# Front projections in two rounded passes, key weights turned on TensorE, expert gate and up products in three rounded passes

## The chip, the cores and the metric

The kernel runs on one core of one Trainium2 chip. The metric is device time in microseconds (us). The core has five engines that matter here: PE (TensorE, matrix products), DVE (VectorE), ACT (ScalarE), POOL (GpSimd) and SP (SyncE, which only issues DMAs). Each works through its own list of instructions in order and waits on semaphores that other engines raise.

## The reference, cut to what matters

`x` is 256 tokens of 256 numbers (batch 8, length 32). Six layers add to it, one after the other. The change touches three of them.

```
# layer 1: quantised attention over 8 groups of 2 heads, head size 128
xq   = fp8(bf16(clip(ln_out / in_scale)))          # one xq for each of qx, k, v, q
q    = ln((xq * in_scale) @ wq.T * w_scale)        # 2048 columns; the same for qx, k (1024), v (1024)
kx   = ln(cond @ w_kv_x[:1024].T)                  # keys of the cross attention, 8 x 512 context rows
x    = x + (self attention | cross attention) @ wproj
# layer 2: state space layer
# layer 3: eight experts of 256 x 256, two of them used by each token
g = silu(x @ Wg[e]); u = x @ Wu[e]; out += ((g * u) @ Wd[e]) * w_e
# layer 4: attention over the context with a mask; layer 5: rotary attention
# layer 6: FFN whose weights come from a table of 16 values: w = lut[idx]
```

## The kernel before

All 256 tokens stay on chip. Every engine has its own hand-written list; nothing is planned by a program at run time. Four stretches follow each other.

**Front.** Six chunks of projection weights of 1024 columns each (`wch`, two buffers) are loaded in turn: two for qx, one for k, two for q, one for v. `project(n)` (L1500) multiplies a chunk with the fp8-rounded input `xs`, which DVE makes in `scaled_input` (last line L1735) for one of four input scales. Both operands are fp32, so that each product of 512 columns is two instructions on PE. The results go to PSUM banks 0 to 3. ACT copies them out in `read_chunk` (L1612) to `raw`. DVE takes statistics of 16 heads in `norm_heads` (L1756 to L1770) while ACT gives the reciprocal root (`act_rstd`, L283 and L284) in the middle. Then DVE scales the first eight heads (L1775) and ACT the other eight in `normalise` (L1632). PE turns the result by transposes (`turn`, L1514), ACT reads it back with the norm's weights (`read_turn`, L1639), and `cross_queries` (L1524, L1529; copied out at L1621) folds the key weights `wkc` into the cross queries. The order of `norm_heads` and of `normalise` is fixed as chunk 0, 1, 2, 3, 4. The key weights are held twice: `wkc`, centred by PE, and `wkT`, the same weights loaded transposed by a second DMA and centred by DVE (L1743 to L1745). At the end `wkT` is split: ACT rounds it to fp32r (`wk_hi`, L1659), DVE subtracts (`wk_lo`, L1800). A product is then taken in rounded passes (hi by hi, hi by lo, lo by hi), each one fp32r instruction.

**Loop.** Eight context rows pass through `loop_pe`: keys and scores in three rounded passes (L429 to L431), mixes in fp32 (L456). In the meantime ACT (`leaf`, L653), DVE (`term`, L660) and accumulating DMAs issued by POOL (L666) build the table weights `lutw` in eight steps of three parts.

**Experts.** `gate_up` (L1043) is eight fp32 products of 256 columns for one expert; ACT takes the silu (L1198), DVE clamps and multiplies (L1325, L1329), `down` (L1054) multiplies back and DVE adds to `x` (L1337). `gate_up(e)` runs one expert ahead of `down(e-1)`. The last two steps of the table weights are spread over experts 2 to 7. Where PE would be idle, `keep_clock` (L364) issues products whose results nobody reads.

**Rest.** Layers 4, 5 and 6, each a chain of norm, turn, product, softmax.

## Time and profile before

| what | value |
|---|---|
| median of 3 runs | 479.61 us (478.98 to 480.41) |
| time of the profiled execution | 483.38 us |
| its span, first to last instruction | 481.6 us |
| PE busy | 450.2 us (93%) |
| DVE busy | 352.0 us (73%) |
| ACT busy | 248.7 us (52%) |
| mean granted TensorE clock | 0.982 |

The profile is of one execution, 3.77 us longer than the median of the runs; 1.78 us of its time lie outside the span. Busy shares are means over stretches with different limits, so that each stretch has to be read by itself. A granted clock of 1.0 is 2.4 GHz, 0.5 is 1.2 GHz.

### The profile page before, as it was taken

The numbers are of one execution on the slowest core, as the hardware profiler recorded it, in microseconds if no ns is written. First come the engines' busy times: TensorE is split into PE (matmuls) and PEld (weight loads), VectorE is DVE, ScalarE is ACT, GpSimd is POOL, SyncE is SP. The second block draws the span as 40 slices with busy tenths as digits, with TensorE's granted clock in tenths as the row PEclk, the third lists the DMA queues.
The fourth block names the chain that finished last, engine by engine and source line by source line (L and its number), as shares of the span: only waits on it lengthen the run. The fifth ranks groups of instructions, "written<-read, shape, count | busy, mean of one in ns | idle before, by whom it ended". The sixth has DMA issues, their size and how long they took to land.

```text
span 481.6 us, 6644 instructions
## 1 busy us (share of the span) xinstructions
PE 450.2 (93%) x2336; PEld 304.9 (63%) x2342; DVE 352.0 (73%) x729; ACT 248.7 (52%) x784; POOL 25.5 (5%) x33
## 2 busy tenths in 40 slices
PE   5987999989999999999999999998888999989897
PEld 2442445667887676767576776856655888536566
DVE  5888495849799869698899989766776468644731
ACT  1465688997553677758986676553020205110120
POOL 0000000000110000101001010100000111100000
PEclk9999799999999999999999999999998999989999
DMA  8167020224201114693448464880068579720000
GB/s 314 82 228 297 0 88 0 79 99 160 82 0 45 44 45 109 136 319 70 110 109 172 111 131 110 177 333 0 1 206 329 176 206 222 166 85 1 1 1 22
DMA packets 14046, 58.57 MB, mean 122 GB/s; under 512 B 1792, under 2 KB 2496, under 8 KB 12480
## 3 DMA queue, kind: packets, MB, share of 16 engines
q1 hardware_dynamic: 10992, 41.66, 23.6%
q0 software_dynamic: 3024, 16.52, 17.6%
q8 instruction: 17, 0.28, 0.2%
q14 instruction: 13, 0.11, 0.1%
HBM read 41.40 MB, written 0.26 MB: 87 GB/s over the span
## 4 chain that ended last, share of the span: by engine, by line
PE 74%; DVE 12%; ACT 10%; issue 2%; DMA 1%; SPq 0%; DVEq 0%; ACTq 0%
PE PS L456 11%; PE PS L429 9%; PE PS L431 8%; PE PS L430 8%; PE PS L1043 6%; PE PS L1529 3%; PE PS L1500 3%; PE PS L476 3%; PE PS L1054 3%; ACT raw_dt.float L1632 3%; PE PS L503 2%; PE PS L1154 2%; ACT raw_dt.float L1612 2%; PE PS L465 1%; PE PS L364 1%
## 5 line engine op out<-in xcount | busy, mean ns | idle before, releaser
L576 ACT ACTIVATE sq_dt.float<-PS 128x128 bf16<-128x128 f32 x256 | 67.3, 281 | 28.9 <-PE PS L431 22.2
L456 PE MATMUL PS<-s_dt.float,ctx_ring_dt.float 128*128 128x512 f32 x128 | 57.7, 593 | 1.3 <-DVE px_dt.float L810 1.3
L429 PE MATMUL PS<-wkc_dt.float32r,ctx_hi_dt.float32r 128*128 128x512 f32 x128 | 53.7, 420 | 1.6 <-ACT sq_dt.float L576 1.2
L576 ACT ACTIVATION_READ_ACCUMULATOR sq_dt.float<-PS 128x1 f32 x256 | 53.8, 211 | 0.0
L431 PE MATMUL PS<-wkc_dt.float32r,ctxT_ring_dt.float32r 128*128 128x512 f32 x128 | 50.4, 393 | 0.0
L430 PE MATMUL PS<-wkT_dt.float32r,ctx_hi_dt.float32r 128*128 128x512 f32 x128 | 50.1, 392 | 0.0
L653 ACT ACTIVATE luttmp_dt.float<-low_bit_dt.float,vec_dt.float,small_dt.float 128x1536 f32<-128x1536 uint8 x24 | 38.5, 1656 | 10.5 <-DMA lutw_dt.float<-luttmp_dt.float 10.5
L1500 PE MATMUL PS<-wch_dt.float,xs_dt.float 128*128 128x512 f32 x96 | 42.2, 594 | 0.7 <-DVE xs_dt.float L1735 0.7
L456 PEld LDWEIGHTS PS<-s_dt.float,ctx_ring_dt.float 128*128 128x128 f32 x128 | 23.6, 190 | 25.0 <-issue 23.0
L660 DVE SCALAR_TENSOR_TENSOR luttmp_dt.float<-idx_dt.float,luttmp_dt.float 128x1536 f32<-128x1536 uint8 x21 | 36.5, 1750 | 0.0
L364 PE MATMUL PS<-consts_dt.float 128*128 128x512 bf16 x116 | 28.9, 404 | 6.0 <-DMA consts_dt.float<-in_consts 5.5
L429 PEld LDWEIGHTS PS<-wkc_dt.float32r,ctx_hi_dt.float32r 128*128 128x128 f32 x128 | 24.0, 187 | 14.1 <-ACT sq_dt.float L576 9.3
L1500 PEld LDWEIGHTS PS<-wch_dt.float,xs_dt.float 128*128 128x128 f32 x96 | 17.8, 190 | 22.3 <-issue 20.3
L666 POOL DMA_DIRECT2D lutw_dt.float<-luttmp_dt.float x21 | 18.3, 871 | 188.2 <-DVE luttmp_dt.float L660 188.2
L431 PEld LDWEIGHTS PS<-wkc_dt.float32r,ctxT_ring_dt.float32r 128*128 128x128 f32 x128 | 24.0, 188 | 5.7
L430 PEld LDWEIGHTS PS<-wkT_dt.float32r,ctx_hi_dt.float32r 128*128 128x128 f32 x128 | 24.1, 188 | 3.6
L797 DVE TENSOR_TENSOR s_dt.float<-s_dt.float,PS 128x2048 f32<-128x2048 f32 x8 | 18.3, 2288 | 10.3 <-PE PS L446 10.3
L364 PEld LDWEIGHTS PS<-consts_dt.float 128*128 128x128 bf16 x122 | 12.1, 103 | 21.0 <-DMA consts_dt.float<-in_consts 5.5
L429 PE MATMUL PS<-A_hi_dt.float32r,ctx_hi_dt.float32r 128*128 128x512 f32 x64 | 25.3, 396 | 0.0
L430 PE MATMUL PS<-A_dt.float32r,ctx_hi_dt.float32r 128*128 128x512 f32 (+1 forms) x64 | 24.9, 390 | 0.0
L431 PE MATMUL PS<-A_hi_dt.float32r,ctxT_ring_dt.float32r 128*128 128x512 f32 x64 | 24.9, 389 | 0.0
L283 ACT ACTIVATE small_dt.float<-small_dt.float 128x2 f32<-128x2 f32 (+1 forms) x12 | 3.7, 304 | 37.6 <-DVE small_dt.float L274 30.1
(272 smaller groups left out, 845.0 us busy)
## 6 DMA issues: line engine op xcount, KB each, us to landing
lutw_dt.float<-luttmp_dt.float POOLq DMA_DIRECT2D x21, 768.0 KB, 6.6
wch_dt.float<-in_chunks SPq DMA_DIRECT2D x6, 1024.0 KB, 5.0
ctxT_ring_dt.float<-in_ctxT SPq DMA_DIRECT2D x8, 512.0 KB, 4.0
ctx_ring_dt.float<-in_ctx SPq DMA_DIRECT2D x8, 512.0 KB, 3.3
keysT_dt.float<-in_ctxT SPq DMA_DIRECT2D x8, 512.0 KB, 7.6
keys_dt.float<-in_ctx SPq DMA_DIRECT2D x8, 512.0 KB, 9.3
luttmp_dt.float<-in_idx SPq DMA_DIRECT2D x3, 768.0 KB, 5.6
zu_dt.float<-in_wproj SPq DMA_DIRECT2D x1, 2048.0 KB, 7.3
```

The costliest lines, as they stand in the source:

```text
L364: nc.tensor.matmul(bank(nb), busy[:, 0:128], busy, start=True, stop=True)
L429: nc.tensor.matmul(o, x_hi, hi[:, c, :], start=c == 0, stop=False)
L430: nc.tensor.matmul(o, x_hi, lo[:, c, :], start=False, stop=False)
L431: last = nc.tensor.matmul(o, x_lo, hi[:, c, :], start=False, stop=c == CT - 1)
L456: last = nc.tensor.matmul(bank(5 + c), keysr[k][:, t, c * 128:c * 128 + 128], sS[k][:, t, :], start=t == 0, stop=t == KT - 1)
L576: last = nc.scalar.activation(sq[:, (4 * hf + g) * D:(4 * hf + g + 1) * D], bank(hf)[:, g * D:(g + 1) * D], ACT.Square, accum_out=ssq[:, k ...
L653: nc.scalar.activation(lutt[:, m, :], low_bit[:, m, :], ACT.Identity, scale=lut_gap[:, k:k + 1], bias=col("lut", 2 * k)).then_inc(lut_leaf, 1)
L660: nc.vector.scalar_tensor_tensor(lutt[:, m, :] if k else lutw[:, m, :], idx[:, m, :], float(2 * k), lutt[:, m, :], ALU.is_equal, ALU.mult) ...
L666: pool.dma_start(lutw[:, m, :], lutt[:, m, :], accum_op=ALU.add).then_inc(lut_added[m], 16)
L797: nc.vector.tensor_tensor(sS[k], sS[k], bank(4).unsqueeze(1).broadcast_to([128, KT, 512]), ALU.subtract)\
L1043: last = nc.tensor.matmul(o[:, m, :], wgu[e % 4][:, i, w0:w0 + 128], hT[:, c, :], start=c == 0, stop=c == CT - 1)
L1500: last = nc.tensor.matmul(bank(q), xs[:, VARIANT[n], c, j * 128:j * 128 + 128], wch[n % 2][:, c, hf * 512:hf * 512 + 512], start=c == 0, s ...
```

## The change

Front: `xs` is no longer multiplied by the input scale. The scale is applied to the weights: ACT writes `wch_hi`, the scaled chunk rounded to fp32r, in two instructions, and DVE writes `wch_lo`, the scaled chunk minus `wch_hi`, in two. `xs` holds fp8 values, which fp32r represents fully, so that a product is two fp32r passes. `wkT` isn't loaded; PE transposes `wkc` in 16 transposes and ACT copies them out. Of 16 heads DVE scales ten, ACT six. ACT's `normalise(2)` and DVE's `norm_heads(2)` stand later in the lists. Experts: ACT rounds gate and up weights of an expert (`wgu_hi`, one instruction of 128x1024), DVE subtracts, and the normed input is split too; each product is three fp32r passes. The last step of the table weights moves behind the experts.

```diff
 def project(n):
     pe.wait_ge(xs_ready, SCALED.index(VARIANT[n]) + 1)
-    pe.wait_ge(ld_chunk[n % 2], 16 * (n // 2 + 1))
+    pe.wait_ge(chunk_hi, n + 1)
+    pe.wait_ge(chunk_split, n + 1)
...
         for c in range(CT):
-            last = nc.tensor.matmul(bank(q), xs[...], wch[n % 2][:, c, ...], start=c == 0, stop=c == CT - 1)
+            nc.tensor.matmul(bank(q), xq, wch_hi[n % 2][:, c, ...], start=c == 0, stop=False)
+            last = nc.tensor.matmul(bank(q), xq, wch_lo[n % 2][:, c, ...], start=False, stop=c == CT - 1)
+def turn_wk():        # PE, behind project(0): 16 transposes of wkc through the PSUM ring, read by ACT
 # ACT
+def split_chunk(n):
+    act.wait_ge(ld_chunk[n % 2], 16 * (n // 2 + 1))
+    if n > 1:
+        act.wait_ge(proj_full, 4 * (n - 1))
+    for c in range(CT):
+        last = nc.scalar.activation(wch_hi[n % 2][:, c, :], wch[n % 2][:, c, :], ACT.Copy,
+                                    scale=col("in_scale", VARIANT[n] * CT + c))
+    last.then_inc(chunk_hi, 1)
-for i in range(8):                       # normalise
+for i in range(2, 8):
+split_chunk(0)
 for i in range(4):
     read_ring("center", i, wkc[:, 2 * i:2 * i + 2, :])
+split_chunk(1)
 read_chunk(0)
+for i in range(4):
+    read_ring("wkturn", i, wkT[...])
 normalise(0)
 read_chunk(1)
+split_chunk(2)
 read_turn(0, zlnT, "qxln_w", "qxln_b")
 normalise(1)
+split_chunk(3)
 read_chunk(2)
 cross_queries(0)
 read_turn(1, zlnT, "qxln_w", "qxln_b")
-normalise(2)
+split_chunk(4)
 read_chunk(3)
 cross_queries(1)
+normalise(2)
+split_chunk(5)
 # DVE
-for c in range(CT):                      # scaled_input: xs times in_scale
-    last = nc.vector.tensor_scalar(xs[:, n, c, :], xs[:, n, c, :], col("in_scale", n * CT + c), None, ALU.mult)
+def split_chunk(n):
+    dve.wait_ge(chunk_hi, n + 1)
+    for c in range(CT):
+        last = nc.vector.scalar_tensor_tensor(wch_lo[...], wch[...], col("in_scale", ...), wch_hi[...],
+                                              ALU.mult, ALU.subtract)
+    last.then_inc(chunk_split, 1)
 scaled_input(0)
-# centring of wkT: reduce, scale, subtract
+split_chunk(0)
+split_chunk(1)
-for i in range(8):                       # norm_heads
+for i in range(10):
 norm_heads(0)
 scaled_input(1)
+split_chunk(2)
 read_turn_cross(0)
 norm_heads(1)
 scaled_input(3)
+split_chunk(3)
+read_turn_cross(1)
 norm_heads(2)
-read_turn_cross(1)
+split_chunk(4)
 scaled_input(2)
 norm_heads(3)
+split_chunk(5)
 # SP
-sp.dma_start(wkT, io["wkT"]).then_inc(ld_wkT, 16)
 # experts, PE
 def gate_up(e, k):
-    pe.wait_ge(ld_e[e % 4], 16 * (e // 4 + 1))
+    pe.wait_ge(gu_split, e + 1)
...
-    last = nc.tensor.matmul(o[:, m, :], wgu[e % 4][:, i, w0:w0 + 128], hT[:, c, :], ...)
+    nc.tensor.matmul(o[:, m, :], wgu_hi[k][:, i, w], hT_hi[:, c, :], start=c == 0, stop=False)
+    nc.tensor.matmul(o[:, m, :], wgu_hi[k][:, i, w], hT_lo[:, c, :], start=False, stop=False)
+    last = nc.tensor.matmul(o[:, m, :], wgu_lo[e % 4][:, i, w], hT_hi[:, c, :], start=False, stop=c == CT - 1)
 # experts, ACT: hi_of_experts(0) and (1) in the state space layer, (e + 2) behind silu(e)
+def hi_of_experts(e):
+    act.wait_ge(ld_e[e % 4], 16 * (e // 4 + 1))
+    if e > 1:
+        act.wait_ge(gu_full, 2 * e - 2)
+    nc.scalar.activation(wgu_hi[e % 2], wgu[e % 4], ACT.Copy).then_inc(gu_hi_ready, 1)
 # experts, DVE: lo_of_experts(0), (1) ahead of the add of layer 2, (e + 2) behind activate(e)
+def lo_of_experts(e):
+    dve.wait_ge(gu_hi_ready, e + 1)
+    nc.vector.tensor_tensor(wgu_lo[e % 4], wgu[e % 4], wgu_hi[e % 2], ALU.subtract).then_inc(gu_split, 1)
-    term(dve, LUT_STEPS + (e - 2) // 3, (e - 2) % 3)
+    if e < 5:
+        term(dve, LUT_STEPS, e - 2)
+for m in range(2):                       # layer 4, while PE makes the readout
+    term(dve, LUT_STEPS + 1, m)
+term(dve, LUT_STEPS + 1, 2)              # layer 5, while PE makes the output product
```

## Rows read from the trace of the kernel before

**Rows 1.** Windows: stretch, length, busy us (instructions) by engine, clock, DMA, GB/s.
```profile
57.00:92.00 35.00, 33.85 (x152) 16.77 (x153) 24.30 (x91) 30.23 (x58) 0.00 (x0) 1.00 0.09 31
151.00:330.00 179.00, 177.39 (x746) 123.27 (x744) 153.27 (x210) 126.78 (x453) 13.36 (x17) 1.00 0.53 136
369.00:415.00 46.00, 45.95 (x199) 39.51 (x201) 29.66 (x58) 12.33 (x14) 6.48 (x7) 0.93 0.75 195
```
**Rows 2.** The chain that ended last, 46 to 73 us: start, length, engine and line.
```profile
46.01 2.29 ACT raw_dt.float L1612 x4
...
48.84 7.45 PE PS L1529 x10
...
58.03 6.87 PE PS L1500 x16
...
65.90 7.08 PE PS L1529 x16
```
**Rows 3.** DVE in order of time: start, length, instruction, idle before and releaser.
```profile
18.82 2.29 DVE L1745 TENSOR_TENSOR wkT_dt.float<-wkT_dt.float,small_dt.float 128x2048 f32<-128x2048 f32 x1
...
48.09 0.62 DVE L1735 TENSOR_SCALAR xs_dt.float<-xs_dt.float,vec_dt.float 128x256 f32<-128x256 f32 x2
...
60.13 0.17 DVE L263 TENSOR_TENSOR small_dt.float<-small_dt.float 128x16 f32<-128x16 f32 x1 [6.91 <-ACT small_dt.float L284]
...
83.83 1.22 DVE L684 TENSOR_TENSOR ctxT_ring_dt.float32r<-ctxT_ring_dt.float,ctx_hi_dt.float32r 128x1024 fp32r<-128x1024 f32 x1
84.96 3.18 DVE L1756 BATCH_NORM_STATS2 small_dt.float<-raw_dt.float 128x6 f32<-128x128 f32 x16
...
89.27 0.17 DVE L1765 TENSOR_SCALAR small_dt.float<-small_dt.float 128x16 f32<-128x16 f32 x1
...
91.06 2.14 DVE L1775 TENSOR_SCALAR raw_dt.float<-raw_dt.float,small_dt.float 128x128 f32<-128x128 f32 x8
```
**Rows 4.** ACT in order of time, front.
```profile
60.97 3.19 ACT L1632 ACTIVATE raw_dt.float<-raw_dt.float,small_dt.float 128x128 f32<-128x128 f32 x8 [0.93 <-DVE small_dt.float L1770]
...
82.53 1.04 ACT L1663 ACTIVATE ctx_hi_dt.float32r<-ctxT_ring_dt.float 128x1024 fp32r<-128x1024 f32 x1
83.48 2.39 ACT L1612 ACTIVATE raw_dt.float<-PS,vec_dt.float 128x512 f32<-128x512 f32 x4
```
**Rows 5.** PE in order of time: a turn, two fp32r keys, two fp32r output products.
```profile
95.40 1.91 PE L1514 MATMUL PS<-consts_dt.float,raw_dt.float 128*128 128x128 f32 x16
...
134.04 0.40 PE L431 MATMUL PS<-wkc_dt.float32r,ctxT_ring_dt.float32r 128*128 128x512 f32 x1
...
136.12 0.39 PE L431 MATMUL PS<-wkc_dt.float32r,ctxT_ring_dt.float32r 128*128 128x512 f32 x1
...
349.11 0.28 PE L488 MATMUL PS<-beta_dt.float32r,catx_dt.float32r 128*128 128x256 f32 x1
...
350.54 0.28 PE L488 MATMUL PS<-beta_dt.float32r,catx_dt.float32r 128*128 128x256 f32 x1
```
**Rows 6.** Windows of short stretches; the granted clock is the third number from the right.
```profile
50.00:53.00 3.00, 3.00 (x5) 1.20 (x4) 2.83 (x15) 1.18 (x3) 0.00 (x0) 0.50 0.00 0
...
372.00:376.00 4.00, 4.00 (x12) 3.14 (x12) 1.86 (x10) 2.08 (x3) 0.00 (x0) 0.56 0.00 0
```
**Rows 7.** DVE, PE and ACT in order of time, layer 2 and the experts.
```profile
363.39 0.69 DVE L1294 TENSOR_TENSOR x_dt.float<-x_dt.float,PS 128x512 f32<-128x512 f32 x1 [1.22 <-PE PS L1020]
...
369.42 10.17 PE L1043 MATMUL PS<-hT_dt.float,gu_a_dt.float 128*128 128x256 f32 x32
...
398.77 1.67 ACT L653 ACTIVATE luttmp_dt.float<-low_bit_dt.float,vec_dt.float,small_dt.float 128x1536 f32<-128x1536 uint8 x1 [4.73 <-DMA lutw_dt.float<-luttmp_dt.float]
...
407.05 3.62 PE L1043 MATMUL PS<-hT_dt.float,gu_b_dt.float 128*128 128x256 f32 x16
410.51 3.62 PE L1054 MATMUL PS<-down_dt.float,moe_dt.float 128*128 128x256 f32 x16
...
414.89 0.87 DVE L1337 SCALAR_TENSOR_TENSOR x_dt.float<-PS,small_dt.float,x_dt.float 128x256 f32<-128x256 f32 x2
```

More of the change, by code:

```diff
@@ L134, in build @@
         tensors = {(name, fp32): tensor(name, fp32) for name in size}
-        for name in ("wkc", "wkT", "ctx_hi0", "ctx_hi1", "ctxT_ring", "A_hi", "A", "catx", "A_first", "beta"):
+        for name in ("wkc", "wkT", "ctx_hi0", "ctx_hi1", "ctxT_ring", "A_hi", "A", "catx", "A_first", "wpx_hi", "xs", "wch",
+                     "wch_hi0", "wch_hi1", "gu_a", "gu_b", "gu_hi", "hT_hi",
+                     "hT_lo"):
             tensors[name, fp32r] = tensor(name, fp32r)
@@ L297, in build, with round_fp8 @@
         t_q = buf("qtmp", 512, skip=768)
-        def round_fp8(step, n, dst):
+        def round_fp8(step, n, dst, out=None):
             step(nc.vector.tensor_scalar(m_bf[:, 0:n].bitcast(u16), y_bf[:, 0:n].bitcast(u16), 0x7F80, None,
@@ L313, in build @@
         wpc = buf("zu", NH, C)
+        wch_hi = [buf(f"wch_hi{k}", CT, 1024, dtype=fp32r) for k in range(2)]
+        wch_lo = [buf("wch", CT, 1024, skip=2048 * k, dtype=fp32r) for k in range(2)]
         raw = [buf("raw", TT, 1024), buf("raw", TT, 1024, skip=2048)]
         RAW_SLOT = {0: 0, 1: 1, 2: 0, 3: 1, 4: 0}
-        lnT, xs = buf("lnT", CT, T), buf("xs", 4, CT, T)
+        lnT, xs = buf("lnT", CT, T), buf("xs", 4, CT, T, dtype=fp32r)
+        xs_wide = buf("xs", 4 * CT * T)
         zlnT, uT, kT, v = buf("zu", 8, T), buf("zu", 8, T, skip=8 * T), buf("kT", G, T), buf("v", TT, 1024)
@@ L343, in build @@
         wpx = buf("A_first", NH, C)
-        wpx_lo, wpx_hi = buf("A_first", NH, C, dtype=fp32r), buf("beta", NH, C, dtype=fp32r)
+        wpx_lo, wpx_hi = buf("A_first", NH, C, dtype=fp32r), buf("wpx_hi", NH, C, dtype=fp32r)
         betaT = buf("qfront", 4, T)
@@ L907, in build @@
         wdn = buf("down", NE, CT * C)
+        wgu_lo = [buf(name, 2, CT * C, skip=2 * k * CT * C, dtype=fp32r) for name in ("gu_a", "gu_b") for k in range(2)]
+        wgu_hi = [buf("gu_hi", 2, CT * C, skip=2 * k * CT * C, dtype=fp32r) for k in range(2)]
+        hT_hi, hT_lo = buf("hT_hi", CT, T, dtype=fp32r), buf("hT_lo", CT, T, dtype=fp32r)
+        hT_hi_ready, hT_split, gu_hi_ready, gu_split = (sem(n) for n in (
+            "hT_hi_ready", "hT_split", "gu_hi_ready", "gu_split"))
         sg = [buf("moe", CT * T, skip=2 * k * CT * T) for k in range(2)]
@@ L1145, in tail_pe @@
             pe.wait_ge(hT_ready, 5)
-            for m in range(3):
+            for m in range(2):
                 pe.wait_ge(lut_added[m], 16 * (LUTN // 2 - 1))
@@ L1367, in tail_dve @@
             step(nc.vector.tensor_tensor(asum[:, 0:TT], asum[:, 0:TT], attends, ALU.mult))
+            for m in range(2):
+                term(dve, LUT_STEPS + 1, m)
             dve.wait_ge(read_full, 1)
@@ L1515, in turn @@
                                                    raw[RAW_SLOT[n]][:, j, c0:c0 + 128], ident)
+                    last.then_inc(ring_full, 1)
+            def turn_wk():
+                pe.wait_ge(ring_read["act"], reads("act", RING_AT["center"] + 4))
+                for i in range(4):
+                    o, c = bank(ring("wkturn", i), 4, D), i // 2
+                    for k in range(4):
+                        last = nc.tensor.transpose(o[:, k, :], wkc[:, 4 * (i % 2) + k, c * 128:c * 128 + 128], ident)
                     last.then_inc(ring_full, 1)
@@ L1643, in _ @@
             act_rstd(act, step, TT, 1)
+            act.wait_ge(ld_const, 32)
+            split_chunk(0)
             for i in range(4):
                 read_ring("center", i, wkc[:, 2 * i:2 * i + 2, :])
+            split_chunk(1)
             read_chunk(0)
+            for i in range(4):
+                read_ring("wkturn", i, wkT[:, i // 2, 512 * (i % 2):512 * (i % 2) + 512])
             normalise(0)
             read_chunk(1)
+            split_chunk(2)
             read_turn(0, zlnT, "qxln_w", "qxln_b")
             normalise(1)
+            split_chunk(3)
             read_chunk(2)
```

77 lines of the change are left out of this document (47 added, 30 removed).

## Prediction

> **What bounds the kernel now.** I read the windows first, to see in which stretch which engine is full; then the chain that ended last, for the stretches that the change touches; then the instructions of DVE, ACT and PE in order of time, for durations and for what ended each wait. In the loop PE is the bound, busy 177.4 of 179 us [rows 1], and nothing there changes. In the front PE is busy too (33.9 of 35 us), but ACT is at 30.2 and DVE at 24.3 of the same 35 [rows 1], and the chain shows why PE's share misleads: from 46 us it goes through ACT's reading of chunk 2, then PE's cross query products, one projection of 6.87 us, products again [rows 2]. Only part of PE's time is on the path, and the change moves work from PE to the two engines that take turns with it. In the experts PE is busy 45.95 of 46 us and DVE has a third free [rows 1].
>
> **Prices.** A projection chunk is 16 instructions in 6.87 us [rows 2]. Afterwards it is 16 fp32r instructions of 512 columns. Nine such starts lie between 134.04 and 136.12 us [rows 5], 0.231 each, so 3.7 us, 3.2 less. An expert's gate and up product takes 3.46 us (407.05 to 410.51 [rows 7]); 24 fp32r instructions of 256 columns at 0.119 (twelve starts from 349.11 to 350.54 [rows 5]) take 2.86, 0.6 less. An ACT copy of 128x1024 holds the engine 0.95 us (82.53 to 83.48 [rows 4]); with a scale column I take 1.0, bounds 0.95 and 1.2, since the column of scale and bias adds more in L1632. Two a chunk are 2.0 us. A DVE subtraction of 128x1024 holds it 1.13 (83.83 to 84.96 [rows 3]); two are 2.26. For the form with a scale column the trace has no row of this size, so I bound it by 0.62 (two such halves as L1735 [rows 3]) and 1.3. A scaled head costs ACT 0.39 [rows 4] and DVE 0.27 [rows 3].
>
> **Front, until 46 us.** DVE loses the centring of wkT (2.29 for its last part [rows 3], 4.8 with the reduction before it) and two times 0.65 for L1735; it gains three splits (6.8) and two heads (0.5). PE's shorter projections take away its 1.5 us of waiting for chunk 0, but it now waits some 2 us for ACT's hi parts of chunks 1 and 2. Net, the second normalisation comes 0.6 later. ACT then has two heads less (0.8) and the hi part of chunk 3 more (2.0) before it reads chunk 2: 46.01 becomes about 47.8, and the cross query products waiting behind that read resume at 50.8 instead of 48.84 [rows 2].
>
> **Front, the second cross queries.** These products ran 7.45 us for ten instructions against 7.08 for sixteen later [rows 2]: the clock was at 0.50 (1.2 GHz) there [rows 6], after PE had stood still until ACT's read (46.01 plus 2.29 and the beta read). The wait before them is longer afterwards, so I charge the same 7.45: 58.2. The turn takes 1.75, the projection of chunk 3 now 3.7, the beta products 1.0, the second cross query products 7.1 and ACT's last read 0.6: 72.4, against 73.5 before. That is a gain of 1 us, but the order of the lists undoes it: `normalise(2)` now stands behind these reads on ACT. DVE's scaling for the third normalisation began at 60.13 [rows 3]; it can begin only at about 72.9 now, 12.8 later, and DVE is idle some 6 us before it. Queued behind that wait on DVE are the split of chunk 4, for which PE's projection waits, the last input rounding, and both remaining normalisations.
>
> **Front, the rest.** From there DVE is a closed line: root step 0.84 and ten heads 2.7, split of chunk 4 2.3, input rounding 3.1, statistics 4.5 (84.96 to 89.44 [rows 3]), ACT's root 0.6, then 0.84 and 2.7, split of chunk 5 2.3, wk_lo 2.2, ctx_lo 1.1, statistics 4.5, root 0.6, 0.84 and 2.7. Sum 31.4, so the last heads are scaled at 104.3; before it was 93.2 (91.06 plus 2.14 [rows 3]), 11.1 earlier. PE wasn't ready then and began the last turn at 95.40 [rows 5]; afterwards PE waits for DVE. So the last turn begins 9.0 later, and ACT, which has half of chunk 5 and A_hi still ahead of it, adds 0.5. Everything behind it (scores, core projection, loop) is in series on PE: front **+9.5 us**. PE's other savings, chunks 0, 1, 2, 4 and 5 and the removed load, fall into its waits. Bounds: with ACT's split at 1.2 each +10.7, DVE's at 1.3 +10.9, DVE's at 0.6 +5.6; drawn in the same way, the order of before gives the end of the core projection within 0.5 us of the trace.
>
> **Layer 2 and experts.** The two subtractions for experts 0 and 1 (2.26 us) stand in a DVE wait of 1.22 [rows 7]: +1.1. The split of the input (ACT 0.55, DVE 0.69) lies beside the router's 1.4 us on PE: 0. The first two experts took 10.0 us [rows 7], as the clock was at 0.56 [rows 6]. At half clock the first is 24 times 0.238, 5.7 us, then the clock is back soon: about 8.7 in all, -1.3. Six more experts at -0.6: -3.5. A LUT step (1.75 us) held DVE while the last down product ended, so that its add began at 414.89, though the product ended at 414.1 [rows 7]: -0.8. The filler products behind it (as many as before) outlast the norm then and give back 0.5. The LUT's last step is still read by ACT (`leaf`) between silus, and there it waits for the accumulating DMA, 4.73 us for the first [rows 7]. With experts at 4.6 us instead of 5.2, landings that stay 7 to 10 us behind their DVE step push the silu of expert 7 back: up to +1.2, I take +0.6. The moved LUT steps lie under the readout product (5.3 us) and the output product (2.0); without that cover they'd cost 1.75 each. Tail: 1.1 - 1.3 - 3.5 - 0.8 + 0.5 + 0.6 = **-3.4 us**.
>
> **A rule against the experts' part.** Each fp32r instruction brings its own weight load. Output products of 256 columns start every 0.119 us with a load each [rows 5], so the loads are hidden. The Trainium skill (TensorE: Matmul & The Clock Gate, "LDWEIGHTS (loading the stationary operand)" and "What overlaps and what doesn't") gives a load its columns over 1.2 GHz and lets it overlap a running product only if the row groups differ, which they don't here. An estimate by that page is 0.107 for load and 0.107 for product, 5.1 us an expert, slower than before by 1.7 each. Its rule becomes a rival below, priced from the windows.
>
> **Sum.** Own time of the profile 483.4 + 9.5 - 3.4 = 489.5 (span 487.7). The median of the runs is 3.8 below the profiled execution; I apply the same change to it: 479.6 + 6.1 = **485.7 us**.
>
> **Rivals.**
> (a) Forecast, DVE's line from 73 us sets the front: 0.60; own range 483 to 488.5.
> (b) The added passes are hidden and PE's saving counts. For: PE is fuller than ACT and DVE [rows 1]. Against: the 12.8 us above need no split to be slow. With both splits free the front is 1.8 shorter than before, so 479.6 - 1.8 - 3.4 = 474.4. It decides on the faster side once the front costs under 3.4, that is when DVE's two instructions a chunk are nearly free. 0.10.
> (c) The clock doesn't fall at the cross queries, or not at the experts: 3.1 us (7.45 against 4.3 for ten instructions) come off: 482.6. For: the phase differs between executions. Against: longer waits of PE. 0.12.
> (d) The clock falls also where it is felt, at chunk 5's projection and the first keys, since PE now waits 5 us before the turns of chunks 2 and 3: up to 3.1 more, 488.8. The Trainium skill (same page, "The HAM clock gate") says that the default is the throttled clock and that activity releases it, which speaks for more such falls. 0.12.
> (e) Weight loads aren't hidden. By the loads' mean in the experts, 39.5/201 = 0.197 us [rows 1], 24 are 4.7, +1.3 on each of eight experts instead of -0.6: +15, 500. 0.02.
> (f) Several errors cancel, no change: 0.04.
>
> Under 0.3% (1.4 us) either way this kernel's measurement can't tell from none. Faster is (b), 0.10, and a part of (f)'s kind, 0.02; same 0.05; slower the rest, 0.83. The range is 480.5 to 490: it leaves out (b), (e) and the far ends.
>
> **What will show it.** Right: ACT's L1632 for chunk 2 starts near 73.7 instead of 60.97; DVE idle about 6 us before it; the last turn near 104; PE's busy share in 57 to 105 well under that of before; chunks' 16 instructions in 3.7 us, but not on the chain; loop of the same length; experts at 4.6 us a step. Wrong: a scaled DVE subtraction far under 1.1 us, or ACT's third normalisation starting before 65 us.

## The result and the profile after

The changed kernel takes 490.19 us (median of four: 487.89, 489.51, 490.87, 492.08), the kernel before beside it 480.01; the ratio is 1.0215, with a 95% interval of 1.0167 to 1.0264. The forecast was 485.7, with a range of 480.5 to 490.0: right in its sign, 4.5 us too low, and the measured time is 0.2 us above the range. The profiled execution is the fastest of the four, 487.89, and stands only 4.5 above the profiled 483.4 of before, while the medians are 10.2 apart. That contradiction between the two profiles and the two medians is what most of the experiments are about.

The head of the page after: the span, the busy time of each engine, and the shares of the chain that ended last.

```profile
span 486.1 us, 6863 instructions
...
PE 434.9 (89%) x2422; PEld 312.0 (64%) x2422; DVE 371.4 (76%) x749; ACT 267.9 (55%) x799; POOL 26.3 (5%) x33
...
PE 64%; DVE 22%; ACT 9%; issue 3%; DMA 2%; DVEq 0%; ACTq 0%
```

The windows that answer to [rows 1] and [rows 6]; the columns are the same.

```profile
57.00:103.00 46.00, 34.03 (x193) 24.59 (x192) 35.91 (x126) 35.12 (x63) 0.00 (x0) 0.85 0.15 54
161.00:340.00 179.00, 177.58 (x747) 123.41 (x745) 153.13 (x209) 126.77 (x453) 13.35 (x17) 1.00 0.53 136
380.00:419.00 39.00, 38.42 (x259) 36.36 (x259) 32.15 (x61) 18.36 (x20) 5.61 (x5) 0.96 0.64 178
...
50.00:53.00 3.00, 2.55 (x3) 1.17 (x4) 1.39 (x2) 2.29 (x5) 0.00 (x0) 0.51 0.00 0
75.00:79.00 4.00, 4.00 (x18) 3.82 (x17) 3.86 (x8) 4.00 (x5) 0.00 (x0) 0.50 0.00 0
```

PE was busy in 97% of the front's window before (57 to 92 us) and is in 74% of it now (57 to 103), at a mean granted clock of 0.85. A stretch at a granted clock of 0.50 is called half clock from here on. The loop is unchanged (177.6 of 179 us). The experts fit in 39 us where they took 46.

The chain of the changed kernel from 62 to 105 us answers to [rows 2, 3]: start, length, what.

```profile
62.91 7.08 PE PS L1588 x16
70.01 0.60 ACT A_dt.float L1690
...
71.14 0.19 DVE small_dt.float L268
...
72.24 2.40 DVE raw_dt.float L1853 x9
74.67 2.48 DVE wch_dt.float32r L1818 x2
...
80.14 3.20 DVE small_dt.float L1834 x16
...
86.19 2.40 DVE raw_dt.float L1853 x9
88.61 2.48 DVE wch_dt.float32r L1818 x2
91.09 2.20 DVE wkT_dt.float32r L1882
...
94.43 3.11 DVE small_dt.float L1834 x16
```

Read it from the top: PE's second cross query products, ACT's last read of them at 70.01, and then almost nothing but DVE to 102.8. This is the line that the forecast drew. And PE at three places, which answers to [rows 2, 5]:

```profile
50.45 6.05 PE L1588 MATMUL PS<-zu_dt.float,wkc_dt.float 128*128 128x512 f32 x10 [5.08 <-ACT beta_dt.float L1658]
...
74.69 3.67 PE L1564 MATMUL PS<-consts_dt.float,raw_dt.float 128*128 128x128 f32 x16 [4.71 <-DVE raw_dt.float L1853]
...
102.85 1.97 PE L1564 MATMUL PS<-consts_dt.float,raw_dt.float 128*128 128x128 f32 x16 [1.83 <-DVE raw_dt.float L1853]
```

A turn takes 1.97 us at full clock and 3.67 behind a wait of 4.71.

### The profile page after: what moved, and what is told of

It is laid out like the page before. It is cut to its first block, busy times and chain, and to the rows that moved or that the text cites. A ratio compares the mean times of both kernels' runs of the same rounds, so it can differ in the third digit from the quotient of the medians.

```text
span 486.1 us, 6863 instructions
## 1 busy us (share of the span) xinstructions
PE 434.9 (89%) x2422; PEld 312.0 (64%) x2422; DVE 371.4 (76%) x749; ACT 267.9 (55%) x799; POOL 26.3 (5%) x33
## 4 chain that ended last, share of the span: by engine, by line
PE 64%; DVE 22%; ACT 9%; issue 3%; DMA 2%; DVEq 0%; ACTq 0%
PE PS L464 11%; PE PS L437 9%; PE PS L439 8%; PE PS L438 8%; PE PS L484 3%; PE PS L1588 3%; DVE small_dt.float L1834 3%; PE PS L511 2%; PE PS L1170 2%; DVE wch_dt.float32r L1818 2%; ACT sq_dt.float L584 2%; DMA lutw_dt.float<-luttmp_dt.float 1%; PE PS L473 1%; ACT raw_dt.float L1701 1%; ACT wch_hi_dt.float32r L1666 1%
## 5 line engine op out<-in xcount | busy, mean ns | idle before, releaser
L372 PE MATMUL PS<-consts_dt.float 128*128 128x512 bf16 x122 | 30.1, 403 | 4.9 <-DMA consts_dt.float<-in_consts 4.9
L437 PEld LDWEIGHTS PS<-wkc_dt.float32r,ctx_hi_dt.float32r 128*128 128x128 f32 x128 | 24.1, 188 | 15.8 <-ACT sq_dt.float L584 10.2
L1564 PE MATMUL PS<-consts_dt.float,raw_dt.float 128*128 128x128 f32 x80 | 14.5, 358 | 14.4 <-DVE raw_dt.float L1853 14.4
L1549 PE MATMUL PS<-wch_hi_dt.float32r,xs_dt.float32r 128*128 128x512 f32 x48 | 21.8, 454 | 5.6 <-DVE wch_dt.float32r L1818 5.6
```

The costliest lines, as they stand in the source:

```text
L372: nc.tensor.matmul(bank(nb), busy[:, 0:128], busy, start=True, stop=True)
L437: nc.tensor.matmul(o, x_hi, hi[:, c, :], start=c == 0, stop=False)
L1549: nc.tensor.matmul(bank(q), xq, wch_hi[n % 2][:, c, hf * 512:hf * 512 + 512], start=c == 0, stop=False)
```

## The experiments

Fifteen runs; two of them repeat an unaltered kernel. The medians of the kernel before beside the four sets are 479.4, 480.4, 479.9 and 481.2 us. "Core product" is the start of the last run of 32 products of the core projection (`project_core`): all that the front costs has happened by then. It is at 139.27 before and at 149.44 after, +10.17.

| kernel | median us | ratio to before (95%) | clock of the profile | core product us | span us |
|---|---|---|---|---|---|
| changed, again | 490.4 | 1.0232 (1.0179 to 1.0286) | 0.951 | 150.61 | 491.6 |
| front alone | 492.1 | 1.0266 (1.0213 to 1.0319) | 0.962 | 150.48 | 490.2 |
| experts alone | 478.5 | 0.9982 (0.9943 to 1.0022) | 0.982 | 139.95 | 477.9 |
| order back | 486.7 | 1.0157 (1.0104 to 1.0210) | 0.968 | 145.76 | 482.1 |
| fillers in the front | 489.8 | 1.0210 (1.0139 to 1.0281) | 0.983 | 149.50 | 488.9 |
| order back and fillers | 485.4 | 1.0127 (1.0049 to 1.0206) | 0.982 | 144.63 | 482.3 |
| no low parts | 483.4 | 1.0094 (1.0055 to 1.0133) | 0.961 | 142.36 | 482.1 |
| high parts on POOL | 495.8 | 1.0352 (1.0298 to 1.0405) | 0.955 | 155.76 | 493.7 |
| before again | 480.5 | 1.0021 (0.9969 to 1.0074) | 0.982 | 138.80 | 481.1 |
| before, two waits filled | 478.1 | 0.9993 (0.9961 to 1.0024) | 0.996 | 136.82 | 475.9 |
| before, all filled | 476.7 | 0.9964 (0.9926 to 1.0001) | 1.000 | 136.92 | 474.5 |
| changed, all filled | 484.3 | 1.0113 (1.0049 to 1.0176) | 1.000 | 147.02 | 482.5 |
| experts alone, filled | 474.0 | 0.9899 (0.9838 to 0.9960) | 0.996 | 137.13 | 472.5 |
| the same, low part late | 476.9 | 0.9950 (0.9917 to 0.9983) | 0.986 | 135.39 | 474.9 |
| experts alone, all filled | 472.4 | 0.9862 (0.9800 to 0.9923) | 0.996 | 138.49 | 472.8 |

These starts count from the first instruction of the profile. PE's first real products (the eight that centre the key weights) start anywhere from 11.8 to 13.2 us, whichever kernel it is, and all that follows moves with them. Counted from those products, the two profiles of the kernel before agree within 0.1 us, and the two of the changed kernel within 0.3:

| profile | first product us | last turn, from it | core product, from it |
|---|---|---|---|
| before | 12.65 | 82.75 | 126.62 |
| before again | 12.20 | 82.70 | 126.60 |
| changed | 11.85 | 91.00 | 137.59 |
| changed, again | 13.24 | 91.17 | 137.37 |
| order back | 12.91 | 86.91 | 132.85 |
| fillers in the front | 13.09 | 91.25 | 136.41 |
| order back and fillers | 11.88 | 88.51 | 132.75 |
| no low parts | 12.38 | 85.00 | 129.98 |
| before, all filled | 13.07 | 79.79 | 123.85 |
| changed, all filled | 12.24 | 89.49 | 134.78 |

So the front costs 10.8 to 11.0 us, not 10.2: the profile of the changed kernel began its work 0.8 us earlier than that of before.

**The changed kernel once more.** No edit.

> The changed kernel once more, unaltered, timed in five rounds and with another profile. Two readings of why its median stood at +10.2 us while its profiled execution stood only +4.5 above that of before. Theory 1 (which execution was profiled): the profile of before was the slowest but one of its four times and that of after the fastest of its four, so a new profile of after shows more clocked-down stretches or longer ones, and comes out at 489 to 492, with the front (start of the loop) later than 161.97 us or a longer tail. Theory 2 (the change's own work varies, a wait that sometimes lasts longer): the new profile shows the same clock within 0.003 and a longer wait at one place. By both the ratio to before stays at 1.017 to 1.026; if it comes out at 1.012 or under, the forecast's +6.1 us was right and the first measurement was not.

Median 490.4. The profiled execution is now the slowest of its six, 493.36 at a clock of 0.951. Theory 1 holds: the same kernel gives profiles 5.5 us apart. Of that 1.2 is there at the core product, and all of it is the later start of the first product; the rest lies in the tail, where the clock fell at 380 to 390, 435 to 440 and 460 to 470 us.

**The parts alone.** Front: the diff without its layer 2, experts and LUT parts. Experts: only these.

> Only the front's part of the change (projections in two fp32r passes, key weights turned by TensorE, heads shared out anew, new list order); layer 2 and the experts as before. Theory of the forecast: +9.5 us on the kernel before, ratio 1.020; the trace of after puts it at +10.2 (start of the loop 161.97 for 151.80). Rival (the front costs more in the median than in the profile, since its waits of 5 us before the turns bring half-clock stretches): +12 us or more, ratio 1.025 or more.

> Only the experts' part (gate and up products in three fp32r passes, input and weights split by ACT and DVE, LUT steps moved); the front as before. Theory of the forecast: -3.4 us, ratio 0.993. By the trace of after, in which the tail lost 10.2 minus 4.5: -5.7 us, ratio 0.988. Rival (the experts' gain in the trace is only that of a luckier clock in that execution): 0 to -2 us, ratio 0.996 to 1.0. The sum of this run's change and that of the front alone should be the whole change if the two parts don't touch each other.

The front alone costs 12.7 us, over its +9.5 and near its rival; the experts alone gain 0.9, near theirs. The sum, 11.8, is within 1 us of the whole (11.0), so no interaction of the two parts shows above the noise of the medians. But the profiles say something else: the core product of the front alone is 11.2 later, and the experts alone, profiled at the same clock as before (0.982), are 3.7 shorter in span. Both parts come out worse in medians than in profiles.

**The order back.**

```
-            split_chunk(4)                 # ACT
+            normalise(2)
+            split_chunk(4)
...
-            read_turn_cross(1)             # DVE
             norm_heads(2)
+            read_turn_cross(1)
```

> The changed kernel with one thing undone: the third normalisation stands again where it stood before, on ACT directly behind its reading of the second turn (ahead of the split of chunk 4) and on DVE ahead of the second cross queries' input. All splits stay. Theory of the forecast (the order of the two lists costs, not the splits): the order laid out with row durations gives 4.2 us less than the changed kernel, 486 where that one has 490, ratio 0.9915 between the two; the wait of DVE before the third normalisation's scaling (6.42 us, ended by ACT) is gone. Rival (the splits' own occupancy of ACT and DVE sets the front): within 1 us of the changed kernel, as DVE's line from there is equally long and the wait only turns up elsewhere.

3.7 us less than the changed kernel beside it (486.7 to 490.4), with 4.2 forecast; core product 3.7 and 4.9 earlier than in its two profiles, 4.7 and 4.5 when counted from the first product. DVE in order of time in this kernel:

```profile
61.62 0.17 DVE L268 TENSOR_TENSOR small_dt.float<-small_dt.float 128x16 f32<-128x16 f32 x1 [4.77 <-ACT small_dt.float L289]
...
82.06 0.18 DVE L268 TENSOR_TENSOR small_dt.float<-small_dt.float 128x16 f32<-128x16 f32 x1 [5.09 <-ACT small_dt.float L289]
```

The third normalisation is scaled from 61.62 on, not from 71.14, but 9.5 us earlier there are only some 4 at the end: a new wait of 5.09 us stands at the fourth one, behind ACT's second cross query reads and what is queued after them. Nor is the wait at the third gone, as was expected: it is 4.77 us, where the changed kernel has 6.42. So the order is one cause, of 4 to 5 us; the other 6 of the front remain.

**Fillers in the front.** `keep_clock` products in PE's waits, each in a bank that the next real product overwrites.

```
+                fill = {0: 9, 2: 20, 3: 25, 4: 8}.get(n, 0)     # turn(n)
+                if fill:
+                    keep_clock(fill, ring(f"turn{n}"))
...
+                    if n == 0 and i == 2:                       # cross_queries(n)
+                        keep_clock(21, 4 + (RING_AT["A0"] + 2) % 4)
```

and 17 in front of `project(2)`. The counts were laid out for the changed kernel's waits; with the order back some waits stand elsewhere.

> The changed kernel with filler products of 0.213 us each in the places where PE waits in the front: 9 before the turn of chunk 0, 17 before the projection of chunk 2, 21 before the third of the first cross query products, 20, 25 and 8 before the turns of chunks 2, 3 and 4. They change nothing else; each is written to a bank that is free and is overwritten by the real product. Theory of the clock (the added waits of PE cost a second time, as the products behind them run at half clock): the 27 to 31 us of half clock in the front fall under 10, the turns take 1.9 us instead of 3.6, the ten products behind the beta read 4.3 instead of 6.1, and the kernel loses 4 to 8 us, to 482 to 486. Rival (the line of DVE from the last cross query read sets the end, and PE's slow products lie beside it): within 1.5 us of the changed kernel, 489 to 491, whatever the clock does.

> The third normalisation back in its old place and the same filler products. If the list order and the clock are two separate causes, their gains add up: the order gave -3.7 us, the fillers what the kernel beside this one shows, so 478 to 482. If the order's gain was only that of fewer half-clock stretches (the wait of PE before the turn of chunk 2 is gone with it), this kernel equals the one with fillers alone within 1 us.

The clock of 57 to 103 us rises from 0.85 to 1.00, and the turns run at full speed:

```profile
57.00:103.00 46.00, 41.63 (x252) 25.40 (x250) 34.49 (x121) 34.58 (x61) 0.00 (x0) 1.00 0.16 58
```

```profile
76.15 1.97 PE L1570 MATMUL PS<-consts_dt.float,raw_dt.float 128*128 128x128 f32 x16 [0.40 <-DVE raw_dt.float L1862]
...
104.34 1.97 PE L1570 MATMUL PS<-consts_dt.float,raw_dt.float 128*128 128x128 f32 x16 [1.88 <-DVE raw_dt.float L1862]
```

Yet the last turn starts at 104.34, as late as in the changed kernel (102.85 and 104.41; 91.2 us behind the first product in all three), and the median is only 0.6 lower, within its spread of 485.9 to 492.9. The rival holds: between 70 and 103 us PE's slow products lie beside DVE's line and cost nothing. The theory that the added waits of PE cost a second time there has fallen. With the order back the kernel takes 485.4 (expected 478 to 482). That is 1.2 less than without fillers, or 2.6 if the longest of its six times (490.4) is left out, and neither is clear of the noise. The ten products behind the beta read, in this kernel and then in the one with the order back, and that one's second cross query products:

```profile
51.69 6.25 PE L1597 MATMUL PS<-zu_dt.float,wkc_dt.float 128*128 128x512 f32 x10 [2.15 <-ACT beta_dt.float L1667]
```

```profile
50.49 4.56 PE L1597 MATMUL PS<-zu_dt.float,wkc_dt.float 128*128 128x512 f32 x10 [2.14 <-ACT beta_dt.float L1667]
...
64.15 10.15 PE L1597 MATMUL PS<-zu_dt.float,wkc_dt.float 128*128 128x512 f32 x16 [2.70 <-DVE zu_dt.float L1873]
```

Behind waits of equal length the ten products ran at half clock in the one profile and at full clock in the other. But with the order back the clock fell later instead, behind an unfilled wait: the second cross query products took 10.15 us for 7.47 in the kernel without fillers. What was won at the first place was lost at the second, and the core product is where it was (132.75 and 132.85 from the first product). So this run does not show what a full clock is worth in the front.

**No low parts.** DVE's `split_chunk` does nothing and the second pass takes the high part again; the kernel leaves out the low parts, so its results are not those of the reference.

> The changed kernel without DVE's subtractions for the low part of the projection weights: the second pass multiplies the high part again, so that PE's work is the same. The low part is left out of the result. Theory of the forecast: the twelve subtractions of 1.13 us stand in DVE's line; by the order laid out with row durations the front gives back 6.3 us, so 484. Rival (the splits hide beside other work, the list order alone costs): under 2 us, 488 to 490.

7.0 us less than the changed kernel's 490.4 (expected 6.3; against the rival's 2). DVE in order of time:

```profile
70.29 0.18 DVE L268 TENSOR_TENSOR small_dt.float<-small_dt.float 128x16 f32<-128x16 f32 x1 [6.40 <-ACT small_dt.float L289]
...
94.54 2.65 DVE L1847 TENSOR_SCALAR raw_dt.float<-raw_dt.float,small_dt.float 128x128 f32<-128x128 f32 x10
```

Its line from the end of that wait to the end of the last heads is 26.9 us; in the changed kernel it is 31.65 (71.14 to 100.14 plus 2.65). The difference of 4.75 is two splits of 2.4 us: one subtraction holds DVE 1.20 us (88.61 to 91.01 for two), where 1.13 was charged.

**High parts on POOL.** ACT's `split_chunk` moved as it is to POOL.

> The changed kernel with the high parts of the projection weights made on POOL, which stands idle in the front, in place of ACT. Theory of the forecast: ACT's 2.0 us a chunk stand in the line (the order laid out with row durations gives 6.2 us back when they are free), so 484 to 485, if POOL makes a chunk in about 4 us. Rival 1: POOL is slower than the projections need (over 8 us a chunk), PE waits for it and nothing is gained or something lost. Rival 2: POOL slows DVE's own instructions beside it, seen as DVE subtractions of over 1.3 us.

495.8. Rival 2 is right. Rival 1 is right in what it says of PE, which waits and loses 5 us, but POOL needs 6.0 us a chunk and not over 8. From the groups by line, first this kernel, then DVE's in the changed one:

```profile
L1777 POOL TENSOR_SCALAR wch_hi_dt.float32r<-wch_dt.float,vec_dt.float 128x1024 fp32r<-128x1024 f32 x12 | 35.7, 2990 | 42.9 <-DMA wch_dt.float<-in_chunks 42.9
```

```profile
L1821 DVE SCALAR_TENSOR_TENSOR wch_dt.float32r<-wch_dt.float,vec_dt.float,wch_hi_dt.float32r 128x1024 fp32r<-128x1024 f32 x12 | 16.6, 1425 | 0.9 <-POOL wch_hi_dt.float32r L1777 0.7
```

```profile
L1818 DVE SCALAR_TENSOR_TENSOR wch_dt.float32r<-wch_dt.float,vec_dt.float,wch_hi_dt.float32r 128x1024 fp32r<-128x1024 f32 x12 | 14.9, 1282 | 2.3 <-ACT wch_hi_dt.float32r L1666 2.1
```

POOL takes 2.99 us where ACT takes 1.14, so the high parts of the first two chunks are ready only at 22.0 us and the first turn starts at 37.7 instead of 29.2; and DVE's subtractions beside it go from 1.28 to 1.43 us. What ACT's part of the front costs was not isolated by this run.

**The waits filled.** The remaining kernels ask why medians and profiles disagree.

```
-                    nc.tensor.matmul(bank(ring(f"A{n}", i)), ...     # cross_queries
+                    o = bank(ring(f"A{n}", i))
+                    if n == 0 and i == 2:
+                        keep_clock(16, 4 + (RING_AT["A0"] + 2) % 4)
...
-            keep_clock(11, 6)                                        # ahead of turn_norm(2)
+            keep_clock(17, 6)
```

All filled: 17 and 18 there, and 4 ahead of each `sc_exp` wait, 4 between the halves of the last mixing, 3 ahead of the output product. The changed kernel has 30 and 24, and its own six places.

> The kernel before with filler products in the two waits of PE after which its profile showed half clock: 16 before the third of the first cross query products and 6 more (17 for 11) ahead of the third norm's turn. It tests the step from the profiled execution to the median. Theory: the executions of the kernel before differ by how many half-clock stretches they have (475.1 us at a mean granted clock of 0.999, 483.6 at 0.982), so with the stretches filled it is 474 to 476 us in every run, at 0.993 or more, with a spread under 3 us. Then its median stands below the profiled execution because most executions lack some of the stretches that the profiled one had, and a kernel that has them in every execution must not be given that discount. Rival (the spread has another cause, such as the start of the transfers): median 478 to 480 and the old spread of 8 us.

> The kernel before with filler products in all the waits of PE after which any of its profiles showed half clock: 17 ahead of the third of the first cross query products, 7 more ahead of the third norm's turn, 4 ahead of each half of the readout's softmax, 4 between the halves of the last mixing and 3 ahead of the output product. Theory of the clock: mean granted clock 0.996 or more in most runs and 474 to 477 us. Rival: the fillers lie in the way and cost what they save, 478 as with two filled waits.

> The changed kernel with filler products in the same waits and in those that the change adds in the front (9, 17, 30, 20, 30 and 14). Against the kernel before with its waits filled (beside this one) it shows the change at nearly equal clock. If the forecast's steps are right (front +9.5, tail -3.4) and only the step to the median was wrong: 5 to 7 us above that kernel, and 3 to 5 below the changed kernel as it is, 485 to 487. Rival (the front is mis-sized by some 3 us, as the front alone measured +12.7): 9 us or more above it.

> The kernel before, unaltered, for another profile of it. By the theory of the median its executions differ by their half-clock stretches: if the profiled one is under 480 us, at least one of the stretches at 45 to 55 us and at 365 to 375 us is absent from it, the ten products behind the beta read take 4.3 instead of 7.45 us if it is the first, and the loop then begins some 3 us earlier. If it is over 483 us, both are there again.

The kernel before, again, in two windows, and the same two with all waits filled (370:374 is not quite the same work, as that kernel is 2 us ahead):

```profile
50.00:53.00 3.00, 3.00 (x5) 1.22 (x4) 2.54 (x14) 1.19 (x2) 0.00 (x0) 0.50 0.00 0
370.00:374.00 4.00, 4.00 (x11) 3.19 (x10) 2.73 (x16) 1.93 (x3) 0.00 (x0) 0.50 0.15 59
```

```profile
50.00:53.00 3.00, 3.00 (x8) 1.33 (x7) 2.90 (x16) 2.33 (x6) 0.00 (x0) 1.00 0.00 0
370.00:374.00 4.00, 4.00 (x20) 3.54 (x19) 2.75 (x10) 2.68 (x4) 1.28 (x2) 1.00 0.54 174
```

The products of the first cross queries, in the kernel before again, before with all filled, and changed with all filled:

```profile
48.36 7.43 PE L1529 MATMUL PS<-zu_dt.float,wkc_dt.float 128*128 128x512 f32 x10 [3.54 <-ACT beta_dt.float L1598]
```

```profile
48.35 5.45 PE L1536 MATMUL PS<-zu_dt.float,wkc_dt.float 128*128 128x512 f32 x12
```

```profile
50.84 4.56 PE L1601 MATMUL PS<-zu_dt.float,wkc_dt.float 128*128 128x512 f32 x10 [0.23 <-ACT beta_dt.float L1671]
```

Ten products take 7.43 us behind an idle wait, and 4.56 behind a filled one. Counted from the first product, the core product comes 2.8 us earlier for it in the kernel before, and 2.8 and 2.6 in the changed one, whose other waits are filled too. That alone is no difference between the two kernels. The difference is how often it happens. The 80 executions of the kernel before that were timed beside the four sets, by mean granted clock:

| clock | executions | us, median (lowest to highest) |
|---|---|---|
| 0.999 or 1.000 | 6 | 475.0 (474.5 to 475.7) |
| 0.993 or 0.996 | 23 | 477.5 (476.1 to 479.1) |
| 0.985 to 0.989 | 30 | 480.9 (479.1 to 482.3) |
| 0.982 or less | 21 | 483.6 (482.5 to 484.9) |

From one end to the other it is 8.6 us of time for about 17 us at half clock (an estimate: 1.8% of the span, twice), just what work at half speed costs. Both profiles of the unaltered kernel, 483.4 and 482.9 us at 0.982, fell in the last row of the table; that the others lack some of the stretches is read from their clocks, and no trace of one of them is here. None of the ten executions of the changed kernel comes near these clocks: they are at 0.951 to 0.965. Against their expectations: with two waits filled the kernel before has a median of 478.1, outside the 474 to 476 expected and inside its rival's 478 to 480; but its spread is 3.7 us and not the rival's 8, and its profile has half clock left behind 445 us. With all filled it is 476.7, as expected. That is 1.7 more than the 475.0 of the unfilled executions at 0.999 or 1.000, so the fillers have a price of their own. The changed one, filled, is at 484.3 (485 to 487), 7.6 above it: over the 5 to 7 of the first theory, short of the 9 of its rival.

**Two terms of the experts' part.** `lo_of_experts(1)` moved from ahead of the `ssm_out_full` wait to behind the low part of the input, with 18 fillers ahead of the third norm's turn where the first kernel has 21; then, in the last kernel, `leaf` at experts 5 to 7 instead of 4 to 6 as well.

> Only the experts' part of the change, as in experts_only, plus filler products in two of PE's waits at which its clock fell in every profile: 16 before the third of the first cross query products and 10 more (21 for 11) ahead of the third norm's turn. Theory of the clock: the ten products at 48.9 us take 4.3 instead of 7.5 and the first two experts about 6.2 instead of 7.5, so 473.5 to 475.5 us where experts_only had 478.5, ratio to before 0.988 to 0.992. Rival (fillers merely shift the fall to a later place): 477 to 479.

> Only the experts' part, with the same fillers (16 and 18), and DVE's subtraction for expert 1 moved from ahead of the state-space sum to behind the low part of the input. Forecast step tested: the two subtractions stand in a DVE wait of 1.22 us and cost 1.1. If that is right, this kernel is 0.8 to 1.2 us below the 474.0 of the experts' part with fillers, 472.8 to 473.2. Against the kernel before with the same fillers (beside this one) the experts' part then shows what it is worth at equal clock: -3.4 - 1.1 by the forecast, so 4.5 us less. Rival (the second expert's product now waits for its low part): no gain, 474 or more.

> Only the experts' part, with the same filled waits, DVE's subtraction for expert 1 late, and the LUT's last step read by ACT one expert later (behind the silus of experts 5 to 7 instead of 4 to 6), so that the silu of expert 7 no longer waits for an accumulating transfer. Forecast steps tested: +1.1 for the two subtractions and +0.6 for the late silu. At equal clock the experts' part is then -3.4 - 1.1 - 0.6 = -5.1 against the kernel before with its waits filled: 470 to 472 us if that one has 475 to 476. Rival: ACT's last read now delays the root of the norm behind the experts, and 473 to 474 results.

The first gives 474.0, within its forecast. The second gave 476.9, a miss: it was to be below the first. Its term is there, from the core product to the x add it takes 224.2 us instead of 225.2, but its profile has half clock at 365 to 370, 415 to 425 and 445 to 455 us, where the first one's has it only at 370 to 375 us. The text recorded ahead of it calls the fillers the same; they are three fewer at the very wait behind which the clock fell at 365, so this run does not test the term by its time. With these waits filled too, the third gives 472.4, the best of all, 1.4% under the kernel before. It was to be 5.1 below the filled kernel before and is 4.3. In its trace the silu of expert 7 no longer waits for the LUT's read (ACT and PE in order of time):

```profile
402.77 0.60 ACT L1226 ACTIVATE moe_dt.float<-PS 128x512 f32<-128x512 f32 x1 [2.17 <-PE PS L1054]
403.26 1.66 ACT L657 ACTIVATE luttmp_dt.float<-low_bit_dt.float,vec_dt.float,small_dt.float 128x1536 f32<-128x1536 uint8 x1
403.99 3.62 PE L1065 MATMUL PS<-down_dt.float,moe_dt.float 128*128 128x256 f32 x16
```

## Why the prediction was right in sign and 4.5 us too low

**Front, until 46 us: right.** ACT reads chunk 2 at 47.53 (forecast 47.8), and the products behind resume at 50.45 (50.8). That this is early is the early start of the profile: with the first product where it was before, they resume at 51.25, in both profiles.

**Front, the second cross queries: right, the cold stretch over-charged.** The ten products took 6.05 and 6.25 us in the two profiles, not 7.45, since the clock came back sooner. That, and the early start, is why the last read ends at 70.6, not 72.4, and DVE starts the third normalisation at 71.14, not 72.9; its idle time before is 6.42 (some 6 forecast). ACT's third normalisation stands at 71.98 (73.7 forecast, 60.97 before). The order back took 3.7 us away where 4.2 was worked out: that the order costs is shown, and so is its size within half a us.

**Front, the rest: the line right, what follows it too small.** DVE's closed line is 31.65 us (31.4 forecast, though the terms as printed add up to 31.8) and ends at 102.79 (104.3); the last turn is at 102.85 (near 104). The splits' share is shown by the run without low parts (7.0 for 6.3). From the first product the last turn comes 8.3 and 8.4 us later than before, where 9.0 was forecast. But behind it I had only 0.5, for ACT's half of chunk 5 and A_hi, and the core product comes a further 2.7 and 2.3 us later: the stretch between the two takes 46.6 and 46.2 us for 43.9. Half clock is a part of that: the granted clock is 0.66 at 110 to 115 us in the one profile, 0.50 at 105 to 110 in the other, and with all waits filled the stretch takes 45.3 for 44.1. How much of the rest is the change is open, since the front of before takes from 43.8 to 45.5 us there in the profiles with filled waits, all at a clock of 1.00. The front as a whole is +11.0 and +10.8 for +9.5, and +10.9 with both clocks at 1.000. The core products of those two, uncorrected:

```profile
136.92 7.07 PE L476 MATMUL PS<-zu_dt.float,catc_dt.float 128*128 128x256 f32 x32
```

```profile
147.02 7.07 PE L484 MATMUL PS<-zu_dt.float,catc_dt.float 128*128 128x256 f32 x32
```

**Layer 2 and experts: right in sign, 1.5 us too hopeful.** DVE, ACT and PE of the changed kernel, the answer to [rows 7]:

```profile
372.30 2.34 DVE L1327 TENSOR_TENSOR gu_a_dt.float32r<-gu_a_dt.float,gu_hi_dt.float32r 128x1024 fp32r<-128x1024 f32 x2
374.56 0.67 DVE L1332 TENSOR_TENSOR x_dt.float<-x_dt.float,PS 128x512 f32<-128x512 f32 x1
...
379.96 0.69 DVE L1337 TENSOR_TENSOR hT_lo_dt.float32r<-hT_dt.float,hT_hi_dt.float32r 128x512 fp32r<-128x512 f32 x1 [0.69 <-ACT hT_hi_dt.float32r L1218]
```

```profile
414.06 1.67 ACT L661 ACTIVATE luttmp_dt.float<-low_bit_dt.float,vec_dt.float,small_dt.float 128x1536 f32<-128x1536 uint8 x1 [1.56 <-DMA lutw_dt.float<-luttmp_dt.float]
415.64 0.57 ACT L1226 ACTIVATE moe_dt.float<-PS 128x512 f32<-128x512 f32 x1
```

```profile
417.45 1.99 PE L1069 MATMUL PS<-down_dt.float,moe_dt.float 128*128 128x256 f32 x8 [0.25 <-DVE moe_dt.float L1369]
```

The two subtractions fill the 1.22 us wait and push the x add: 225.1 us behind the core product, 224.1 before, so +1.0 for +1.1. The LUT's read waits for its transfer and the silu of expert 7 for it, as forecast. An expert takes 4.55 us a step (4.6 forecast; loads are hidden, 0.118 a product), so rival (e) is out. The Trainium skill (TensorE: Matmul & The Clock Gate, "What overlaps and what doesn't") lets a load run beside a product only where their row groups differ; here both use all rows, and the trace disagrees with it. From the x add to the end, with both clocks at 1.000, it is 110.4 for 113.4 us: -3.0, not -4.5. The traces account for about these 1.5. The input's low part holds PE up for 0.33 (I had 0). The six fillers that the filled changed kernel has more than the filled one before hold PE until 376.2, with the norm's result ready at 375.9: another 0.3 or so, which the unfilled kernel does not pay. And PE, done with the first two experts' products, waits 0.95 us for DVE, which it did not before:

```profile
374.02 1.89 PE L1054 MATMUL PS<-down_dt.float,moe_dt.float 128*128 128x256 f32 x8
```

```profile
385.73 1.96 PE L1069 MATMUL PS<-down_dt.float,moe_dt.float 128*128 128x256 f32 x8 [0.95 <-DVE moe_dt.float L1373]
```

The first silu stands behind the router's small steps on DVE and ACT's table load, which did not get shorter (383.14, 4.3 us behind the start of the first expert's products; before, at 371.64, 4.6). So at full clock the first two experts gain 0.1 us, where twice the 0.6 of the others would be 1.2.

**The step that failed.** "The median of the runs is 3.8 below the profiled execution; I apply the same change to it." The profiled 483.4 was an execution at a clock of 0.982, with half clock in the first cross queries, in the first experts and once in the tail, at 425 to 430 us; by its clock, the median execution of before has fewer such stretches. The changed kernel's waits of PE are longer, and none of its ten executions is above 0.965. It got a discount of 3.8 that it never earns. By its own time I had forecast 489.5, and the medians are 490.2 and 490.4: of the 4.5 us, 3.8 are this step and 0.7 the sizes.

The filled kernels say it another way. With all waits filled, the kernel before falls from 480.4 (median of the 80) to 476.7 and the changed one from 490.4 to 484.3: a full clock is worth 3.6 before and 6.1 after, in both less what the fillers cost. That is 2.5 of the 4.1 us missing from +6.1, and the other 1.5 is sizes: at equal clock the change costs 7.6 in medians. In the spans of the two profiles it is 8.0 (+10.1, +0.9, -3.0; forecast +9.5, +1.1, -4.5), and 8.8 with the front counted from the first product. So the sizes were too small by 0.7 to 2.7 us, by which pair one takes, above all behind the last turn and in the first two experts; the runs don't settle it more finely.

**Rival (d)**, at 0.12, is right in part. The clock fell at the turns and at chunk 5's projection as it says, and there it cost nothing. It also fell behind the last turn, at 105 to 115 us, which the rival names as the first keys: there it costs some 1 us at most (46.6 and 46.2 us for 45.3 filled), not 3.1. Rival (b) is out: without DVE's subtractions alone the kernel comes 7 us lower, so they are far from hidden. Rival (c) is out, as the ten products began at half clock in both profiles, though for less long than before; and (f), as the kernel did change.

## What to carry to other kernels

A pass moved from PE to ACT and DVE is free only where those engines don't take turns with PE: draw the closed line of waits first, with every instruction queued on it, and price the list order apart from the new work, as each was a good part of the loss here. Before you compare two profiles, look where each starts its first real work (here 11.8 to 13.2 us), and before you set a profile against a median, look at the granted clock of each execution; a profile at 0.982 and a median near 0.986 differ by 3 us with nothing changed, and a change that lengthens PE's waits takes the lucky executions away. Where an engine's slow stretch lies beside another engine's line, curing it brings nothing, and where it lies on the line, products written to a bank about to be overwritten are a cheap cure, as long as they are counted for the waits of the very kernel they stand in: with the experts' part alone, and two of its list positions moved, they gave 472.4 us, 1.4% under the kernel before.

## What the runs showed of the hardware

The granted clock fell after PE waits of 2.0 to 8.5 us in which it did nothing, but not each time: behind waits of 2.15 and 2.14 us, ahead of the same ten products, it was at half in one profile and at 1.00 in the other. The wait ahead of those products filled with 16 to 30 products of 0.213 us left it at 1.00 in seven of the eight profiles that have them. Between the executions of the kernel before, time grew by the full half of the time at half clock (8.6 us for some 17); between 70 and 103 us of the changed kernel, beside DVE's line, half clock cost nothing. In the experts' part with 16 fillers and 10 more, the mean clock of five of six executions was 0.996; the kernel before reached that in under a quarter of its own. A scaled copy of 128x1024 to fp32r takes POOL 2.99 us and ACT 1.14 us, and DVE's three-operand instruction of that size went from 1.28 to 1.43 us beside POOL's. An fp32r product of 256 columns with a new load each starts every 0.118 us, one of 512 columns every 0.23.
